# Grouped attention in a decoder kernel: scores made twice, row extremes turned and subtracted by a product of 32 rows

## The reference, cut to what matters

```
qh = q.reshape(B, S, 8, 4, 8)   # q = layernorm(x); 32 query heads of 8, four to a KV head
kh = vh = context as 8 heads of 8
scores = einsum('bkgsd,bktd->bkgst', qh, kh) / sqrt(8)
weights = softmax(scores)
out = einsum('bkgst,bktd->bkgsd', weights, vh)
x = x + out
```

## Time and profile before

| | us |
|---|---|
| median of 3 runs | 1464.92 (1464.51 to 1465.16) |
| the profiled execution | 1456.42 |
| its span | 1454.3 |
| PE busy | 1255.8 (86%) |
| DVE busy | 989.9 (68%) |
| ACT busy | 841.6 (58%) |
| POOL busy | 652.3 (45%) |

### The profile page before, as it was taken

One profiled execution on the slowest core, in us unless ns is written; L12 is line 12 of the kernel. 1 busy time (PEld: TensorE's weight loads), 2 busy tenths in 40 slices (PEclk: granted clock), 3 DMA queues, 4 the chain that ended last, 5 costly groups with the idle time before them and its releaser, 6 DMA issues. The chain is left out here.

```text
span 1454.3 us, 26646 instructions
## 1 busy us (share of the span) xinstructions
PE 1255.8 (86%) x7918; PEld 982.7 (68%) x7918; DVE 989.9 (68%) x1910; ACT 841.6 (58%) x2172; POOL 652.3 (45%) x737
## 2 busy tenths in 40 slices
PE   6995899998998997369899999999987988969998
PEld 4673555556788886347777777777774565648887
DVE  5998788885775455878777877787763666643443
ACT  5443899996355545456666666666652655543232
POOL 2002666665225265476666666676663333320000
PEclk9997899998999998679999999999996999989999
DMA  8000333331014523300000000000000000000000
GB/s 320 16 0 15 88 87 88 88 70 59 0 30 121 142 80 136 112 39 1 1 1 0 0 0 0 0 0 0 0 2 4 4 3 4 2 1 1 15 14 30
DMA packets 41574, 57.22 MB, mean 39 GB/s; under 512 B 5856, under 2 KB 34528, under 8 KB 40224
## 3 DMA queue, kind: packets, MB, share of 16 engines
q1 hardware_dynamic: 38048, 46.90, 10.5%
q0 software_dynamic: 3456, 9.44, 2.5%
HBM read 38.50 MB, written 9.44 MB: 33 GB/s over the span
## 5 line engine op out<-in xcount | busy, mean ns | idle before, releaser
L2332 ACT ACTIVATE wi_weights<-wi_psum,wi_bias,wi_scale 128x128 f32<-128x128 f32 x256 | 113.9, 454 | 117.6 <-DVE wi_bias L2442 117.6
L929 ACT ACTIVATE gq_weights<-gq_psum,gq_least 128x128 f32<-128x128 f32 x512 | 151.8, 526 | 2.0 <-DVE gq_least L977 2.0
L2107 POOL TENSOR_TENSOR wi_straight<-wi_straight,wi_crossed 128x512 f32<-128x512 f32 x80 | 103.6, 1295 | 10.8 <-DVE wi_crossed L2428 10.8
L977 DVE TENSOR_REDUCE gq_least<-gq_psum 128x4 f32<-128x512 f32 x128 | 86.0, 685 | 26.7 <-PE gq_psum L854 26.0
L2095 POOL TENSOR_TENSOR wi_scratch<-wi_sums,wi_eps 128x4 f32<-128x4 f32 x80 | 35.0, 438 | 132.5 <-DVE wi_sums L2411 131.1
L2096 POOL TENSOR_TENSOR wi_scale<-wi_scratch,minus_half 128x4 f32<-128x4 f32 x80 | 84.6, 1057 | 6.3
L2433 DVE TENSOR_REDUCE wi_top<-wi_psum 128x4 f32<-128x512 f32 x64 | 44.0, 687 | 63.6 <-PE wi_psum L2222 63.6
L2231 PE MATMUL wi_psum<-wi_weights_t,wi_values 128*128 128x512 f32 x128 | 68.8, 619 | 20.5 <-DVE wi_weights_t L2449 20.5
L862 PE MATMUL gq_psum<-const,gq_weights 128*128 128x128 f32 x512 | 79.0, 277 | 1.3 <-ACT gq_weights_t L937 0.3
L2858 DVE TENSOR_REDUCE cr_top<-cr_psum 128x4 f32<-128x512 f32 x64 | 43.6, 681 | 45.5 <-PE cr_psum L2673 45.5
L862 PEld LDWEIGHTS gq_psum<-const,gq_weights 128*128 128x128 f32 x512 | 63.3, 142 | 14.5 <-DVE gq_weights_t L990 4.2
(11 more groups left out here) (404 smaller groups left out, 3925.8 us busy)
## 6 DMA issues: line engine op xcount, KB each, us to landing
gq_keys<-in_ctx_keys_dram SPq DMA_DIRECT2D x16, 512.0 KB, 3.9
gq_keys_diagonal<-gq_key_parts SPq DMA_DIRECT2D x64, 128.0 KB, 4.0
slot_y<-ex_s_out SPq DMA_DIRECT2D x20, 256.0 KB, 2.2
x<-in_x_dram SPq DMA_DIRECT2D x4, 512.0 KB, 7.7
gate<-in_gate_dram SPq DMA_DIRECT2D x2, 1024.0 KB, 5.3
up<-in_up_dram SPq DMA_DIRECT2D x2, 1024.0 KB, 7.7
down<-in_down_dram SPq DMA_DIRECT2D x2, 1024.0 KB, 10.1
egu<-in_egu_dram SPq DMA_DIRECT2D x1, 2048.0 KB, 14.1
```

Of the source, the lines that this page charges most:

```text
L929: e = act.activation(weights[:, u % RINGS, j * P:j * P + P], ps[:, u % 4, j * P:j * P + P], ACT.Exp, bias=least[:, u % 4, j:j + 1], scale= ...
L977: dve.tensor_reduce(least[:, u % 4, :], rows(u), AX.X, ALU.min).then_inc(topped, 1)
L2107: added_up = pool.tensor_tensor(straight[:, at], straight[:, at], crossed[:, at], ALU.add)
L2332: act.activation(weights[:, g % 2, j, :], ps[:, SC + g % 2, j * P:j * P + P], ACT.Exp, bias=bias[:, g % 2, j:j + 1], scale=scale[:, g, j:j ...
```

## The change

A step is now half a batch, four KV heads, `n` = 0 to 31. The stage keeps two sets of scores:

- The first scores have tokens in the partitions, as before (128 rows, 512 columns, four KV heads with one query head each, two banks). They serve only for the row minima.
- The minima of a whole batch (32 per token) are split into high and low parts, placed in a mostly zero tensor of 128x512, turned by four transposes and copied by ACT (`least_t`).
- The shifted scores have context tokens in the partitions: four products of 32 rows (keys stationary, turned queries moving, 512 columns), each in its own row strip of the array and its own bank, then four products of 32 rows of a constant -1 table with the turned minima into the same banks.
- ACT's exponent has no bias and one instruction covers a bank of 128x512; its result is `weights_t`, and the attend product reads it. The turns of the weights and their copies are gone.
- ACT makes all copies of turned queries. DVE makes none.
- All loops over batches are written out. PSUM: two banks for first scores, four for shifted scores, one for all turns, one for results.
- The keys: repeated over the query heads only in rows, 128 KB a batch in place of 512; four `kbd` buffers, each a quarter of a former one; loaded in three DMAs for all batches.
- POOL prepares queries three batches ahead and keys four ahead; `fold_ffn0` moves from the last batch to batches 13 and 14.

```diff
+    VW, HALVES, LEAD = 32, 2 * NB, 3
+    SLOTS, KEYS = 6, 4
+    TR, O = 6, 7
 ...
 POOL
+            scale_of(pool, own, net, scratch, aggregated, rstd_ready, 0, 1, WIDEN)
+            split_h(0)
+            scale_of(pool, own, net, scratch, aggregated, rstd_ready, 1, NB, WIDEN)
+            pool.memset(least_parts[:].bitcast(F32), 0.0).then_inc(ones_set, 1)
+            pool.wait_ge(net.keys_in[1], 16)
+            next_keys(1)
+            split_h(1)
+            next_keys(2)
+            split_h(2)
 ...
 PE
+            def shifted_scores(n):
+                pe.wait_ge(least_taken, n // 2 + 1)
+                pe.wait_ge(tables_set, 2)
+                for v in range(4):
+                    g = 32 * v
+                    need(pe, weighed, 4 * (n - 1) + v + 1)
+                    pe.matmul(ps[:, 2 + v, :], kbd[n // 2 % KEYS][g:g + 32, n % 2, v, :], h_t[g:g + 32, n % SLOTS, :],
+                              start=True, stop=False)
+                for v in range(4):
+                    g = 32 * v
+                    pe.matmul(ps[:, 2 + v, :], minus[g:g + 32, n % 2, :], least_t[g:g + 32, n // 2 % 2, :],
+                              start=False, stop=True).then_inc(shifted, 1)
+            for n in range(-LEAD - 1, HALVES + 1):
+                ahead = 0 <= n + LEAD < HALVES
+                if 0 <= n < HALVES:
+                    shifted_scores(n)
+                if ahead:
+                    scores(n + LEAD, 0)
+                    scores(n + LEAD, 1)
+                if n % 2 and 0 <= n + 1 < HALVES:
+                    turn_least((n + 1) // 2)
+                if n >= 1:
+                    attend(n - 1)
+                if ahead:
+                    scores(n + LEAD, 2)
+                if n + LEAD + 1 < HALVES:
+                    turn_head(n + LEAD + 1)
+                if ahead:
+                    scores(n + LEAD, 3)
+                if n >= 1:
+                    turn_out(n - 1)
 ACT
+            def weigh(n, v):
+                act.wait_ge(shifted, 4 * n + v + 1)
+                need(act, attended, n - 1)
+                act.activation(weights_t[:, 4 * (n % 2) + v], ps[:, 2 + v, :], ACT.Exp,
+                               scale=-1.0).then_inc(weighed, 1)
+            for n in range(-LEAD - 1, HALVES + 1):
+                if 0 <= n < HALVES:
+                    for v in range(3):
+                        weigh(n, v)
+                if n % 2 and 0 <= n + 1 < HALVES:
+                    take_least((n + 1) // 2)
+                if 0 <= n < HALVES:
+                    weigh(n, 3)
+                if n >= 1:
+                    take_out(n - 1)
+                if n + LEAD + 1 < HALVES:
+                    take_head(n + LEAD + 1)
 DVE
+            for n in range(-LEAD, HALVES + 1):
+                if n >= 2:
+                    divide(n - 2)
+                for j in range(4):
+                    if n + LEAD < HALVES:
+                        minimum(n + LEAD, j)
+                    if j == 1 and n >= 0 and n % 2 == 0 and n // 2 + 3 < NB:
+                        normalise(n // 2 + 3)
+                    if j == 2 and n >= 5 and n % 2 and n // 2 < NB:
+                        measure(n // 2 - 2)
+                if n % 2 == 0 and n + LEAD < HALVES:
+                    split_least((n + LEAD) // 2)
+                if n == HALVES - 3:
+                    for b in range(NB - GB):
+                        dve.bn_aggr(net.mean_var[:, b, :], net.stats[:, b, :]).then_inc(aggregated_ffn, 1)
+                if n == HALVES:
+                    dve.wait_ge(rstd_ffn, 1)
+                    for b in range(6):
+                        normalise_ffn(dve, net, b)
```

More of the change, by code:

```diff
@@ L881, in turn_out @@
                 for j in range(4):
[L882 removed]
+                    mm = pe.transpose(ps[:, O, j * P:j * P + P], out_t[:, n % 2, j * P:j * P + P], ident)
                 mm.then_inc(out_turned, 1)
[L885 to L900 removed]
@@ L902, in _ @@
-            for c in range(2):
-                head(0, c)
-            scores(0, 0, 0)
-            pairs(pe, one)
-            t, s = NB - 1, 1
-            for u in range(U - LAG, U):
-                turn(t, s, u)
-            attend(t, s, 1)
-            for c in range(2):
-                turn_out(t, c)
+            for n in range(-LEAD - 1, HALVES + 1):
[17 more added lines that the diff above has]
+                    turn_out(n - 1)
@@ L913, in _ @@
         @block.scalar
         def _(act):
-            def take_head(t, s, c):
-                if place(half, t, c)[0] == 0:
-                    act.wait_ge(turned, half(t, c) + 1)
-                    need(act, scored, U * (t - 2) + 4 * c + 4)
-                    act.activation(h_t[:, s, 4 * c:4 * c + 4].rearrange("p u t -> p (u t)"), ps[:, bank(half, t, c), :],
-                                   ACT.Copy).then_inc(taken[0], 1)
-            def weigh(t, s, u):
-                act.wait_ge(topped, U * t + u + 1)
-                if not (isinstance(t, int) and t == 0 and u < RINGS):
-                    bt, _, bu = earlier(t, s, u, RINGS, U)
-                    act.wait_ge(turned, unit(bt, bu) + 1)
-                for j in range(4):
-                    e = act.activation(weights[:, u % RINGS, j * P:j * P + P], ps[:, u % 4, j * P:j * P + P], ACT.Exp,
-                                       bias=least[:, u % 4, j:j + 1], scale=-1.0)
-                e.then_inc(weighed, 1)
@@ L945, in one @@
-            def one(t, s, first, last):
-                for u in range(U):
-                    if u >= LAG or not first:
-                        take(*earlier(t, s, u, LAG, U))
-                    if u in (3, 5) and not last:
-                        take_head(t + 1, 1 - s, u // 4)
-                    weigh(t, s, u)
-                    if u in (0, 4) and not first:
-                        take_out(t - 1, u // 4)
-            for c in range(2):
-                take_head(0, 0, c)
-            pairs(act, one)
```

379 lines of the change are left out of this document (160 added, 219 removed).

## The result

The changed kernel takes 1428.47 us (median; 1426.62 to 1435.70) against 1464.72 of the kernel before on the same chip: ratio 0.975, interval 0.9723 to 0.9777. Forecast were 1423 us and 1408 to 1456. In the profiled execution (1428.85 us, span 1427.0) the third stage starts at 309.4 us where I had forecast 301.9 and where it started at 344.3 before: the second stage gave 34.9 us, not 42. The medians are 36.3 us apart, 5.5 less than forecast.

The account below looks back on a forecast made before the run. ACT was taken as the second stage's bound. First exponent 154.5 + 2 + 31 x 4.40 + 9 = 301.9 against 344.3, 42 us less, so 1464.9 - 42 = 1423 us; range 1408 to 1456.

Parts of the forecast that it names:

- Shifted scores: PE's eight 32-row products per half batch, in four strips and four banks: 0.65 us, bounds 0.6 to 3.2.
- The even step: Half batch without the turn of the extremes: PE waits for ACT's copy of the output, 4.03 us.
- sign of error: Wrong if score products wait more for DVE than ACT, strips start 0.21 apart, or clock below 1.00 after 165 us.
- The odd step: Half batch with the turn and copy of the extremes, ended by PE's turn of the output: 4.53 us.
- waits that meet: Allowance of 0.12 us a step for PE, ACT and DVE being near one another, raising 4.28 to 4.40.
- The folds: POOL's folding, moved earlier beside exponents: if uncovered, at most its overlap with the last two steps, 3 us.
- The start: Stretch up to the second stage's first exponent: 154.5 us (152 to 158), 10 us later than before.
- cold first step: First step of the new pipeline at the cold clock: adds 2 us.
- Strips in series: Rival: 32-row products go one after the other, 5.68 us a step, 1462 us, slower with unhidden weights; chance 0.09.
- Latency chain: Rival: three nearly equal engines in strict order stall one another, 5.2 us a step, 1448 us; chance 0.17.
- The clock: Rival: clock falls to 1.2 GHz, PE's issue becomes some 7.8 us a step, 1528 us; chance 0.02.
- Load-bound: Rival: the output's copy never delays PE, 4.1 us a step, gain 52, 1413 us; chance 0.10.

Follow-up runs that it names:

- the one-strip run: Changed kernel with all eight 32-row products of a half batch on the first row strip; one execution takes 1475.14 us.
- the second profile of the same kernel: Changed kernel unedited, timed and profiled again beside the reordered one; median 1436.07 us, ratio 0.9783 to the kernel before.
- the versions without holds: Changed kernel with DVE's later normalisation in odd steps and POOL's add ahead of the head split, alone (1421.52 us) or with start and folds also reordered (1420.61 us).
- the version with all edits: Changed kernel with start reordered, normalisation in odd steps, folds waiting for the extremes' split, and add ahead of the head split; median 1420.61 us, ratio 0.9684.
- the first repair: Changed kernel with DVE's normalisation of a later batch in odd steps instead of even ones; 1458.3 us.
- the same repair with the add moved: Changed kernel with DVE's later normalisation in odd steps and POOL's add issued ahead of the head split; 1421.52 us, ratio 0.970.

## Why the prediction was right, and where it was off

**The bound and its change: right.** ACT left the bound by load and the step was set near 4.4 us by the order of the three engines; ACT at 75%, exponents 0.60 long, 0.5 apart. What the exponents cost before was overstated: 9.5 us a batch by their busy time, 8.0 by their starts (32 of 0.25). With four copies of 0.5 in half a batch that gives the measured 6.0, and the sum of the new kernel does not use the 9.5.

**Shifted scores: right.** Forecast 0.65, measured 0.67 (235.88 to 236.55), from a row of another format and width; the one-strip run shows that this rests on the strips. The weights of the second four (PEld at 235.99) load while the first four multiply (235.88 to 236.39). By the rule of the Trainium skill weighed in the prediction ("TensorE: Matmul & The Clock Gate", Part 3), that a weight load overlaps a running product only when the row group differs, the block would be 0.84, an estimate; the trace shows 0.67, with loads on the same row groups.

**The even step: right, in size and reason.** Forecast 4.03, with PE waiting for ACT's copy of the output; measured 3.96. The copy ends 3.33 into the step (forecast 3.4), PE sees it 0.05 later, as forecast, and is free for the next step 0.59 behind that. What is not so is the size of PE's wait: PE reaches this point at about 3.34 and loses some 0.04 us, so that the even step is as nearly PE's own queue. I had named as a sign of error that score products wait for DVE more than for ACT. In the table they do (24.3 us against the 5.6 of the turned output), yet it costs nothing: the 0.84 us ahead of the score product's weights at 238.20 pass while the attend product runs (237.21 to 238.21), and PE has no gap there. The condition was badly put; a wait in the row of the weight loads counts only if PE is later for it.

**The odd step: the term DVE's split was mis-sized.** I put 0.5 us (bounds 0.4 to 1.0) from a reciprocal and a division, which read PSUM. The split goes from SBUF to SBUF and took 1.15 + 0.22 with POOL's head split beside it, outside my bounds; odd steps are 4.85 and not 4.53. Undisturbed it is 0.20 + 0.22, and then the odd step is 4.45, ended by the copy as forecast. The allowance of 0.12 for waits that meet, argued from nothing in particular, covered it by luck: (3.96 + 4.85) / 2 = 4.41. The Trainium skill has rules for this, which I did not use ("SBUF — State Buffer", Who interferes with whom): a DVE cast can run in a mode that uses the ports shared with GpSimd, if its operands allow it, and then whichever of the two was issued first keeps them for its whole instruction; a DVE instruction with two SBUF inputs contends with a GpSimd instruction that reads SBUF; on trn2 a reduction never contends. The runs agree for the first two: conversion 0.20 to 1.12 us beside L773, subtraction 0.22 to 1.93 beside L1019. The reductions stay at 0.686, but they read PSUM, so no run here tests the third. That the ports are the reason is the skill's word; the runs show the hold and what it costs.

**The folds: a cover that I did not price against the split.** I let them cost at most 3 us, as overlap on POOL. They cost 5.8 through DVE in this profile, and about 1 more in the cold step behind; in the second profile of the same kernel, with steps of 6.15 and 7.31, 3.8 and nothing behind.

**The start: a wait left out.** The chain that I added up ran over POOL's queue to batch 1; that DVE stands ahead of its first reductions in a wait for the scale of all blocks was not in it. 2.85 us of the miss; with that wait gone the first exponent is at 154.03, against 154.5. The 2 us for a cold first step did not come: PE's transposes at 155.49 are already shorter (0.93 us for four, against 1.06 at 153.70), the granted clock is 1.00 from 157 us on, and the first two steps take 8.8.

**Rivals.** Strips in series: excluded by the trace and priced by the one-strip run. Latency chain of 5.2: not so, but the holds are a piece of it. The clock: 1.00 from 157 to 275 us, 0.84 between 275 and 286 with the folds, 0.50 from about 290 to 303, 1.00 in the last 6 us of the stage. So it was below 1.00 after 165 us, which I had named as a sign of error, but only at the end; its price was a few microseconds, part of it in the next stage, which I had assumed to meet the same state. Load-bound, 4.1: the versions without holds run at (3.96 + 4.45) / 2 = 4.2, with PE busy 119.69 of 120 us in one of them. In the odd steps of the version with all edits the turn follows the last score product by 0.41 in place of 0.31, so PE's own queue would take about 4.35 and 3.93, 4.14 on average: an estimate, and near what I had put. A small slip: steps of 4.2 to 4.8 are 1417 to 1435 us by the sum of the prediction, not 1419 to 1438.

Open: why the third stage differs by 12.3 us behind its first 72 between two executions of the kernel before; and whether the cold end of the second stage could be kept warm, and whether that would give back the microseconds in the third, which wasn't tried.

## What to carry to other kernels

When work leaves a bound engine, price each new small DVE instruction from SBUF to SBUF by what POOL runs beside it, and not by its length alone: a hold of 0.95 us here met some 0.5 us of slack and lengthened every second step by 0.40. To move an instruction away from such a hold, follow every queue that waits for it: the first repair cost 23 us through an add in POOL's queue, and the same repair with the add moved gained 11, more than half of it because the folds then missed the split as well. A wait in the table counts where the engine itself is later for it, which only the order of time shows: 0.84 us ahead of a weight load cost nothing, and 0.20 ahead of another marked what ended the step. To price an instruction in a queue, take the distance between starts and not the busy time: 0.25 against 0.298 us here.

## What was new about the hardware

- A stage of unchanged code started slower behind a stage in whose last 20 us the granted clock had fallen to 0.50: 0.69 to 0.79 in its first 40 us, against 0.83 (nine profiles against two; the cause is argued).
- DVE's 128x32 conversion from SBUF to SBUF: 0.20 us alone, 1.12 (median) beside POOL's second instruction of the head split, 1.29; its 128x32 subtraction: 0.22 alone, 1.93 beside a POOL instruction of 1.98. Each ends with POOL's, within 0.1 us. Reductions out of PSUM show no such change.
- Four 32-row fp32r products of 512 columns in four strips and four banks: four records in 0.50 us, 0.34 from one set of four to the next. In one strip 1.20 and 1.04.
- An exponent of 128x128 costs ACT's queue 0.25 us with a bias from SBUF and 0.157 without, one of 128x512 without a bias 0.48.
